# A decoder layer in one kernel: a later wait for the rows of ones, a new order in the context stage, and products in its last two waits

## The reference

```
x = x + attention(layernorm(x))            # 16 heads of 16, rotary, softmax over 1024 keys, projection
x = x + cross(ctx, ctx, layernorm(x))      # one head of 256, 77 keys per batch
x = x + experts(layernorm(x))              # 8 experts, each takes its 512 best tokens, 256 -> 1024 -> 256

cross: kp = k Wk^T;  vp = v Wv^T + bv;  qp = q Wq^T + bq
       probs = softmax(qp kp^T / 16);  out = (probs vp) Wo^T + bo
experts: rms norm, logits, softmax, top 512 tokens per expert, gelu MLP, weighted scatter-add
```

## Time and profile before

| | |
|---|---|
| median of 3 runs | 1216.48 us |
| profiled execution | 1217.81 us |
| its span, first to last instruction | 1215.9 us |
| TensorE busy | 1083.3 us (89%) |
| VectorE busy | 1020.6 us (84%) |
| ScalarE busy | 767.3 us (63%) |
| GpSimd busy | 354.3 us (29%) |
| attention | from 109 to 805 us of the span |
| context stage | from about 805 to 936 us |

### The profile page before, as it was taken

The page is one execution under the profiler, slowest core; times in us unless marked ns, Lnnn a source line. Parts: engine busy times, 40 slices in busy tenths (PEclk is TensorE's granted clock), DMA queues, the critical chain, the costliest instruction groups (busy, mean ns, idle before and its releaser), DMA issues. The chain is left out here.

```text
span 1215.9 us, 24367 instructions
## 1 busy us (share of the span) xinstructions
PE 1083.3 (89%) x8474; PEld 595.2 (49%) x8474; DVE 1020.6 (84%) x2144; ACT 767.3 (63%) x930; POOL 354.3 (29%) x316
## 2 busy tenths in 40 slices
PE   5888899999999998999999999988874049999996
PEld 4775333333333332333333333356763038888996
DVE  7998899999999997999999999547866976766752
ACT  4552188888888886788888787843554014656553
POOL 2756922211220221122112000022200022865673
PEclk9997599999999998999999999999975559999998
DMA  6785764513441441344134000045522022554442
GB/s 232 245 249 188 179 108 95 94 25 68 77 73 22 77 77 32 59 77 77 25 69 77 16 16 16 16 143 194 174 70 92 0 70 59 154 147 110 112 108 31
DMA packets 84694, 114.08 MB, mean 94 GB/s; under 512 B 25057, under 2 KB 57569, under 8 KB 84577
## 3 DMA queue, kind: packets, MB, share of 16 engines
q1 hardware_dynamic: 66288, 69.83, 19.3%
q0 software_dynamic: 15024, 36.17, 16.5%
q10 hardware_dynamic: 3264, 6.55, 1.5%
HBM read 73.31 MB, written 38.27 MB: 92 GB/s over the span
## 5 line engine op out<-in xcount | busy, mean ns | idle before, releaser
L807 DVE TENSOR_REDUCE b_max_halves<-banks 128x1 f32<-128x512 f32 x1024 | 626.9, 680 | 19.8 <-PE banks L875 19.6
L747 ACT ACTIVATE b_probs<-banks 128x1024 f32<-128x1024 f32 x512 | 520.4, 1026 | 154.4 <-PE banks L926 154.3
L875 PE MATMUL banks<-b_k,b_q 62*128 62x512 f32 x1024 | 400.4, 471 | 10.7 <-PEq L101 5.3
L926 PE MATMUL banks<-b_q,b_k 64*128 64x512 f32 x1024 | 386.7, 457 | 8.4 <-DMA b_k<-b_minus 4.5
L897 PE MATMUL banks<-b_probs,b_v 128*17 128x256 f32 (+1 forms) x3840 | 315.0, 401 | 0.2 <-ACT b_probs L747 0.2
L926 PEld LDWEIGHTS banks<-b_q,b_k 64*128 64x128 f32 x1024 | 157.3, 186 | 230.8 <-issue 177.9
L875 PEld LDWEIGHTS banks<-b_k,b_q 62*128 62x128 f32 x1024 | 162.5, 190 | 43.0 <-DVE b_max_halves L807 36.1
L897 PEld LDWEIGHTS banks<-b_probs,b_v 128*17 128x17 f32 x3840 | 64.1, 95 | 165.5 <-issue 97.8
L549 POOL TENSOR_TENSOR b_att<-b_out,b_rec_spread 128x512 f32<-128x512 f32 x32 | 41.1, 1283 | 307.3 <-DMA b_rec_spread<-reciprocals 307.1
L481 POOL DMA_DIRECT2D b_q<-q_stacks x60 | 31.8, 532 | 236.2 <-PE banks L897 222.7
L1812 DVE TENSOR_TENSOR e_hTl<-e_hT,e_hTh 128x512 fp32r<-128x512 f32 x64 | 47.6, 745 | 47.7 <-ACT e_hT L1556 47.7
(11 more groups left out here) (252 smaller groups left out, 1474.1 us busy)
## 6 DMA issues: line engine op xcount, KB each, us to landing
e_w<-in_w SPq DMA_DIRECT2D x16, 1024.0 KB, 7.6
q_stacks<-a_parts SPq DMA_DIRECT2D x32, 256.0 KB, 4.2
k_stacks<-a_parts SPq DMA_DIRECT2D x32, 256.0 KB, 4.0
b_q<-q_stacks POOLq DMA_DIRECT2D x30, 256.0 KB, 6.2
b_k<-k_stacks POOLq DMA_DIRECT2D x30, 256.0 KB, 7.3
v_tiles<-a_v ACTq DMA_DIRECT2D x8, 544.0 KB, 3.3
b_q<-b_max_rows SPq DMA_DIRECT2D x256, 2.0 KB
b_rec_spread<-reciprocals SPq DMA_DIRECT2D x128, 32.0 KB, 1.8
```

The costliest lines, as they stand in the source:

```text
L747: nc.scalar.activation(pr[:, S % NP, u], ps[:, 2 * u:2 * u + 2, :], ACT.Exp, scale=D ** -0.5).then_inc(s_ex[u], 1)
L807: v.tensor_reduce(mxp[:, (k // NB) % 2, s, p, t, kh:kh + 1], ps[:, bank(last), :], AX.X, ALU.max)\
L875: nc.tensor.matmul(ps[:, bank(last), :], qs[g][stack, p, at:at + P], ks[g][stack, p, CH * kh:CH * kh + CH], start=True, stop=True).then_in ...
L926: return nc.tensor.matmul(ps[:, 2 * u + s, :], ks[g][stack, u, P * kt:P * kt + P], qs[g][stack, u, CH * h:CH * h + CH], start=True, stop=True)
```

## The change

In `attend`, TensorE waits for a group's ones at the start of that group and no more at the start of the group before.

In `cross_attend`, four things:

- VectorE makes the probabilities after the whole square root and -mean times the root, and no longer between its last two Newton rounds.
- ScalarE normalises chunk s - 1 before it copies the transposed probabilities of chunk s - 2.
- TensorE makes the transposes of k = 0 ahead of the value product and those of k = 1 after it.
- At the start of the steps 8 and 9 TensorE waits until the last x1 is made and runs seven products of 128x128 by 128x256 into bank 4; no one reads them.

```diff
-                    if first and h == 0 and g < NG - 1:
-                        pe.wait_ge(s_one[g + 1], 32)
+                    if first and h == 0 and g:
+                        pe.wait_ge(s_one[g], 32)
...
@@ ScalarE, each step s
-                if 0 <= s - 2 < J:
-                    act.wait_ge(s_tp, s - 1)
-                    copy(pT[:], ps[0:SK, 2, :]).then_inc(s_tpe, 1)
                 if 0 <= s - 1 < J:
                     j = s - 1
                     act.wait_ge(s_st, s)
                     normalise(xn[:, j % 2], x1[:, j % 3], j, 0, s_na)
+                if 0 <= s - 2 < J:
+                    act.wait_ge(s_tp, s - 1)
+                    copy(pT[:], ps[0:SK, 2, :]).then_inc(s_tpe, 1)
...
@@ VectorE, each step s
                 newton(v, chain, *root)
-                if 0 <= s - 1 < J:
-                    probabilities(s - 1)
                 newton(v, chain, *root)
                 v.scalar_tensor_tensor(nm[:, s, u], mv[:, s, u, 0], -1.0, rs[:, s, u], ALU.mult, ALU.mult)\
                     .then_inc(s_st, 1)
+                if 0 <= s - 1 < J:
+                    probabilities(s - 1)
...
@@ TensorE
+            def idle_products(n):
+
+                for _ in range(n):
+                    mm(ps[:, 4, 0:C], wp[:, 0, 0:P], wp[:, 0, :], start=True, stop=True)
+
             for s in range(NS):
+                if s >= J:
+                    pe.wait_ge(s_m1e, 2 * J)
+                    idle_products(7)
...
+                def transposes(j, k):
+                    for t in range(NT):
+                        last = mm(ps[:, k, P * t:P * t + P], xn[:, j % 2, t, P * k:P * k + P], ident[:],
+                                  is_transpose=True, start=True, stop=True)
+                    return last
+                if 0 <= s - 1 < J:
+                    j = s - 1
+                    pe.wait_ge(s_na, s)
+                    if j == 0:
+                        pe.wait_ge(s_kqe, KC + 1)
+                    after(pe, s_tne, j)
+                    transposes(j, 0)
...
                 if 0 <= s - 1 < J:
-                    j = s - 1
-                    pe.wait_ge(s_na, s)
-                    if j == 0:
-                        pe.wait_ge(s_kqe, KC + 1)
-                    after(pe, s_tne, j)
-                    for k in range(KC):
-                        for t in range(NT):
-                            last = mm(ps[:, k, P * t:P * t + P], xn[:, j % 2, t, P * k:P * k + P], ident[:],
-                                      is_transpose=True, start=True, stop=True)
-                    last.then_inc(s_tn, 1)
+                    transposes(s - 1, 1).then_inc(s_tn, 1)
```

## The result

The changed kernel took 1213.3 us (median of 14 runs, 1205.47 to 1215.86), the kernel before 1217.22 us (14 runs, 1215.57 to 1222.82). The ratio is 0.995, with a 95% interval from 0.9936 to 0.9964: 4 to 8 us faster, and within the 1% of no change. It is the ratio of the means, 1212.36 and 1218.14 us; the medians lie 3.9 us apart. The forecast was 1210.2, with a range from 1204.5 to 1216.5, and 7.6 us under the execution it was reckoned from.

The account below looks back on a forecast made before the run. VectorE's row was taken to bound full-clock context steps, TensorE half-clock ones. Gains of 0.5 (ones), 2.0 (context order) and 5.1 (products) sum to 7.6, so 1217.8 becomes 1210.2 us; range 1204.5 to 1216.5, narrower range 1207.5 to 1213.

Parts of the forecast that it names:

- Ones later: Start of attention: the first score product's wait ends sooner, by the maxima rows; 0.5 us, bounds 0 and 1.4.
- Square root before the probabilities: Context stage, VectorE: root work fills its 0.77 us hole; 0.63 us less per step, 0.3 lost to a new wait.
- Halved transposes: Context stage, TensorE: four of eight xn transposes fill its 0.68 us wait; hidden at full clock, a gain at half clock.
- the half-clock step: Context stage step of 15.15 us at granted clock 0.66, bounded by TensorE; forecast gain 0.7 us.
- The step from 896.83: Context stage step starting at 896.83 us in the profile before; forecast gain 0.3 us.
- GpSimd's add: Bias add in three context steps holds VectorE's variance pair; hold grows 0 to 0.34 us, leaving 0.2 us gain each.
- my rows: The context stage steps listed from the profile before, starting at 846.76 us, over which the forecast was summed.
- T: Moment in a context step when its probabilities are ready and TensorE starts to transpose them.
- Seven products: Last two context steps: unread products take 3.2 us in a 3.65 us wait and keep full clock; gain 5.1 us.
- The clock in the middle: Middle context steps: the forecast kept the one step at granted clock 0.66, with no further fall.
- rival 1: Context stage: full clock spreads to the step that ran at 0.66; 3.1 us more gain, 1207.2 us; chance 0.15.
- rival 3: Middle of the context stage: the clock falls once more, costing 3.4 us, so 1213.7 us; chance 0.15.

Follow-up runs that it names:

- e1: Only the later wait for the ones, added to the kernel before; median 1217.90 us, ratio 1.0008.
- e2: The new order on VectorE, ScalarE and TensorE alone, in the kernel before, without later ones or unread products; median 1222.94 us, ratio 1.0023.
- e4: The changed kernel with 24 transposes in place of each seven products; median 1214.17 us, ratio 0.9968.
- e6: The changed kernel without GpSimd's bias add, the bias left out; median 1205.68 us, ratio 0.9886.
- e3: The seven unread products alone, in the last two steps of the kernel before; median 1213.29 us, ratio 0.9967.
- e5: VectorE's new order alone, in the kernel before; median 1215.10 us, ratio 0.9963.
- e11: The changed kernel itself, timed again on another chip; median 1207.05 us of 6 runs, ratio 0.9908.
- e8: The changed kernel with unread products also at the start of steps 3 to 7; median 1206.54 us, ratio 0.9898.
- e7: The changed kernel with each GpSimd bias add cut into four quarters; median 1206.18 us, ratio 0.9908.

## Why the prediction was right, and where it was not

- *Ones later, 0.5:* the mechanism is right, the maxima rows end the wait now. The first score product waits 3.32 us for them in the changed kernel:

```profile
141.64 0.76 PE L926 MATMUL banks<-b_q,b_k 64*128 64x512 f32 x1 [3.32 <-DMA b_q<-b_max_rows]
```

  The size stays open: 0.37 us between the means of four and of ten profiled executions whose ranges overlap (e1).
- *Square root before the probabilities, 0.63 less 0.3:* right. The hole is closed; the wait it brings before the second half is 0.16 us, not 0.3. A step without bias add takes 11.13 us, against 11.44 in the old order (e1): 0.31 less, where I forecast 0.33.
- *Halved transposes:* 0.4 in step 8, as forecast (10.76 in place of 11.17). In the middle 0.05. For the half-clock step I took 0.7, the whole filled wait: at the same clock of 0.66 such a step takes 14.85 us instead of 15.15, 0.3 less. The step from 896.83, for which I took 0.3, takes 11.13 instead of 11.18: behind a half-clock step VectorE had already done a part of its row (9.55 us busy instead of 10.19).
- *GpSimd's add:* I let the hold grow by 0 to 0.34 us and took three steps. In these the add costs 0 to 0.4 us (11.14 to 11.54 in e2 and e4, against 11.13). I missed the step ahead of my rows, which takes 13.12 us with the hold and 10.92 without (e6). Before, it took 12.62, and its rows were:

```profile
839.45 2.35 POOL L1155 TENSOR_TENSOR c_xb<-c_x,c_bp 128x1024 f32<-128x1024 f32 x1 [6.41 <-DMA c_x<-in_x]
...
840.29 1.60 DVE L1225 SCALAR_TENSOR_TENSOR c_ve<-c_mv,c_eps 128x4 f32<-128x4 f32 x2
...
846.76 0.66 PE L1321 MATMUL banks<-ident,c_probs 128*77 128x128 f32 x4 [1.60 <-DVE c_probs L1202]
```

  The variance pair starts 6.15 us after T in both kernels; VectorE doesn't come earlier in this step. It is the add that starts later after T, 6.21 us instead of 5.31, and so falls on the pair with its whole length. With halved transposes it starts 5.81 to 6.32 us after T in all seven profiled kernels that have the whole new order and the add, with the old order of ScalarE and TensorE 4.44 to 5.33 in the six others. So in this step the whole new order loses 0.5 us (13.08 in e2, against 12.60 to 12.62 before and in e1 and e3), where VectorE's order alone wins 0.5 (12.12 in e5). My sum put this step at nothing. Why the add comes later after T is open.
- *Seven products, 5.1:* right. 3.22 us each time (forecast 3.2), and steps of 10.76 and 8.49 us (forecast 11.15 less 0.4, and 8.5). e3 has them alone: 4.0 us over all runs (1.3 to 6.6), and 4.8 in these two steps against the execution that I reckoned from.
- *The clock in the middle:* this is the step that failed. I kept one half-clock stretch, as in the profile, and gave one more of 3.4 us a chance of 0.15. In the profiled execution there were two, 4.3 and 3.2 us over the same steps before, and neither is the step in which the clock fell before (it took 10.93 us now). Only 7 of the 20 runs of the changed kernel are at 1208.5 or below. At full clock throughout it takes about 1207 (e4's execution, e11's low runs), which was my rival 1 (1207.2); the first set's median of 1213.3 is what my rival 3 gave (1213.7). My argument against rival 3 was that the stretch between large products gets no longer. It is wrong where the add holds VectorE: the pause ahead of T grew from 1.60 us to 2.72 in the changed kernel, because the step became 0.5 us longer and TensorE fills its earlier waits in it. Whether that pause is why the clock fell is open (e6).

The number came out inside the range, but with luck. The forecast was the case of one stretch. The medians of the two sets lie on both sides of it, at 1213.3 and 1207.05, and the first is just outside the narrower range that I gave for the forecast itself (1207.5 to 1213). The count of half-clock stretches is a larger term than any but the seven products, and I could not have fixed it from one execution.

## What to carry to other kernels

Count the half-clock stretches in several runs before you price an edit of 5 us: here one stretch is worth 3 to 5 us, more than a better order of one stage. Work that keeps TensorE busy in a wait, and fits into it at full clock, paid in the last two steps (e3); in the middle it cost nothing, and a gain was not shown (e8). When the order of a step changes, look in every step, the first too, for the operation of another engine that the bounding one now meets: here a bias add that came 0.9 us later after T fell on VectorE's small operations with its whole length.

## What the runs showed of the hardware

24 transposes in the place of seven products held the granted clock at 1.00 in the same two steps (e4). A GpSimd add of 128x1024 held small VectorE operations until its end to within 0.1 us (2.42 instead of 0.24 us); cut in four it held four operations for a quarter each (0.65 instead of 0.17), among them two with one tensor input (L60, L61). Pauses of TensorE ahead of T of 1.60 us (before), 2.44 (e7), 2.60 (e4) and 2.69 (e2) passed, and the step behind ran at 1.00, while the clock fell behind pauses of 2.72 (changed), 2.34 (e11) and 1.98 (changed), and in a step behind one of 0.61 (before); so the length of the pause ahead of T is not all that decides. What does is open. Open is also why e2 was slower than e5, and whether the 6 us between the changed kernel's two sets are the chip's or chance.
